# Norms of the context's keys taken during the self-attention tiles, and kept for the cross-attention tiles

## What is computed

```
q  = _ln(_fp8_linear(ln_out, wq).reshape(b, s, g, hpg, d))     # 16 heads of d=128
k  = _ln(_fp8_linear(ln_out, wk).reshape(b, s, g, d))          # 8 heads
v  = _fp8_linear(ln_out, wv)
core = _gqa(q, k, v)                                            # self attention
qx = _ln(_fp8_linear(ln_out, wqx).reshape(b, s, g, hpg, d))
kx, vx = jnp.split(einsum('bsi,oi->bso', cond, w_kv_x), 2, -1)
kx = _ln(kx.reshape(b, sc, g, d))                               # keys of the context
xout = _gqa(qx, kx, vx)                                         # cross attention
catq = _div_clamp_fp8(concat([core, xout]), proj_smooth)
x = x + tanh(g) * einsum(catq, wproj) * scale
```

## Time and profile before

| what | us |
|---|---|
| median of 3 runs | 717.38 (716.02 to 719.93) |
| the profiled execution | 718.68 |
| its span | 717.0 |
| attention part, first self score to the last cross tile's start | 204.9 to 552.6 |
| one self tile (tiles 2 to 6) | 22.7 and 23.0 in turn |
| tiles 7 and 8 | 24.9 each |
| cross tiles 9 to 14 | 22.6, 20.6, 21.2, 22.7, 21.2, 22.6 |
| busy, share of the span | PE 85%, DVE 71%, ACT 53%, POOL 51% |

### The profile page before, as it was taken

The page is one execution under the profiler, slowest core; times in us unless marked ns, Lnnn a source line. Parts: engine busy times, 40 slices in busy tenths (PEclk is TensorE's granted clock), DMA queues, the critical chain, the costliest instruction groups (busy, mean ns, idle before and its releaser), DMA issues.

```text
span 717.0 us, 10737 instructions
## 1 busy us (share of the span) xinstructions
PE 607.7 (85%) x3738; PEld 487.4 (68%) x3738; DVE 511.7 (71%) x959; ACT 380.9 (53%) x674; POOL 366.0 (51%) x306
## 2 busy tenths in 40 slices
PE   4686986589677999999997898889888989999995
PEld 2453433353455888788876787778777878888885
DVE  4679777688259689888896688998998683533333
ACT  1445767765376465655575656665665424433321
POOL 2421265000367566565667766686775643755521
PEclk9897998789699899999998969999998999999999
DMA  7950211004502010010352031220220100221001
GB/s 234 309 198 0 104 73 59 31 36 156 162 11 79 1 60 30 30 61 0 118 198 84 29 113 50 74 69 22 74 74 16 45 1 1 67 66 31 1 1 59
DMA packets 36246, 50.68 MB, mean 71 GB/s; under 512 B 8289, under 2 KB 22497, under 8 KB 36193
## 3 DMA queue, kind: packets, MB, share of 16 engines
q1 hardware_dynamic: 36192, 50.00, 21.2%
HBM read 37.41 MB, written 12.58 MB: 70 GB/s over the span
## 4 chain that ended last, share of the span: by engine, by line
PE 41%; DVE 17%; issue 10%; ACT 3%; POOL 3%; DVEq 0%; POOLq 0%; ACTq 0%
PE g_proj L2077 7%; PE g_proj L2001 6%; PE g_scores L2035 4%; DVE g_yb L1623 4%; DVE g_ve L1591 3%; PE g_turn L2024 2%; PE g_proj L457 2%; PE g_proj L458 2%; PE g_proj L459 2%; PE g_op L472 2%; PE g_op L474 2%; PE g_op L473 2%; PE g_op L2059 2%; POOL g_rs L1495 2%; DVE g_big L1641 1%
## 5 line engine op out<-in xcount | busy, mean ns | idle before, releaser
L1495 POOL TENSOR_TENSOR g_rs<-g_ve,neg_half 128x4 f32<-128x4 f32 x96 | 101.9, 1066 | 85.1 <-DVE g_ve L1591 75.4
L1591 DVE TENSOR_REDUCE g_ve<-g_sq 128x4 f32<-128x516 f32 x96 | 64.3, 680 | 41.3 <-ACT g_sq L1807 32.9
L2001 PE MATMUL g_proj<-w_hi,g_xqc 128*128 128x512 f32 x192 | 85.7, 446 | 7.9 <-POOL g_xqc L1490 6.0
L1506 POOL TENSOR_TENSOR g_cat<-g_big,g_kb 128x1024 fp32r<-128x1024 bf16 x32 | 68.3, 2134 | 39.4 <-DVE g_big L1641 39.4
L2024 PE MATMUL g_turn<-ident,g_qn 128*128 128x128 f32 x384 | 60.5, 286 | 25.0 <-DVE g_qn L1597 15.0
L2001 PE MATMUL g_proj<-w_lo,g_xqc 128*128 128x512 f32 x192 | 79.9, 416 | 0.0
L1807 ACT ACTIVATE g_sq<-g_proj 128x512 f32<-128x512 f32 x80 | 47.8, 597 | 51.6 <-PE g_proj L2001 49.3
L2035 PEld LDWEIGHTS g_scores<-g_qkT 128*128 128x128 f32 x512 | 65.1, 205 | 12.4 <-issue 11.7
L2035 PE MATMUL g_scores<-g_qkT 128*128 128x64 f32 x512 | 66.1, 286 | 7.4 <-DVE g_ex L1607 7.4
L500 POOL TENSOR_TENSOR m_h_lo<-m_h,m_h_hi 128x512 fp32r<-128x512 f32 x32 | 41.3, 1294 | 59.8 <-ACT m_h_hi L487 59.8
L2024 PEld LDWEIGHTS g_turn<-ident,g_qn 128*128 128x128 f32 x384 | 46.2, 147 | 36.9 <-DVE g_qn L1597 17.5
(11 more groups left out here) (229 smaller groups left out, 1680.4 us busy)
## 6 DMA issues: line engine op xcount, KB each, us to landing
kvx_rows<-f_kept SPq DMA_DIRECT2D x32, 256.0 KB, 2.4
g_kraw<-kvx_rows SPq DMA_DIRECT2D x16, 256.0 KB, 3.3
g_v<-kvx_rows SPq DMA_DIRECT2D x8, 512.0 KB, 4.9
m_raw<-in_L_W SPq DMA_DIRECT2D x16, 256.0 KB, 3.3
c_raw<-in_L_wqT SPq DMA_DIRECT2D x4, 512.0 KB, 9.2
f_w_ctx<-in_L_wkvxT SPq DMA_DIRECT2D x4, 512.0 KB, 7.8
x_raw<-in_L_wqxT SPq DMA_DIRECT2D x4, 512.0 KB, 3.8
c_praw<-in_L_wprojT SPq DMA_DIRECT2D x4, 512.0 KB, 6.1
```

What stands on the lines that cost most here:

```text
L1495: G.tensor_tensor(rs[:, i % 2, :], ve[:, i % 2, :], k["half"][:, 0:4], ALU.pow).then_inc(q["rs_done"], 1)
L1506: G.tensor_tensor(cat[:, h].rearrange("p h (b s) -> p b h s", b=2), big[:, h, :].rearrange("p (b h s) -> p b h s", b=2, s=SEQ), kb[:, h, : ...
L1591: V.tensor_reduce(ve[:, i % 2, :], sq[:, i % 2], AX.X, ALU.add).then_inc(q["ve_done"], 1)
L2001: last = T.matmul(bank(n, i)[:], xqc[:, n % 2, view * KT + c_, :], w[:, c_, :], start=c_ == 0 and part == 0, stop=c_ == KT - 1 and part == 1)
```

## The change

The norms of the context's keys no longer belong to the cross tiles. During self tile n = 0 to 7 the keys of context tile n are loaded once more from `kvx_rows` (512 KB in one transfer, into a new buffer `ksq`), ACT squares all eight heads in place (`key_squares`), DVE sums them (`key_sums`, into a column block of `kve`), and POOL takes the power (`key_rstd`, into `krs`), where they stay. Cross tiles norm only the four chunks of queries; their keys are still loaded and multiplied as before, by `krs`. The parity of `sq`, `ve` and `rs` now counts only chunks that are measured (`measured`), so the waits between them shift. To make room for the new buffers, `big` is gone: `lift` writes back into `yb`, and the wait on `cat_done` moves from `power` to `unload`.

```
+        ksq, kve, krs = sb("ksq", [P, KV, D + 1]), sb("kve", [P, TILES * KV]), sb("krs", [P, TILES * KV])
...
+                def norm_keys(n):
+                    if n > 0:
+                        sp.wait_ge(q["kve_done"], n)
+                    sp.dma_start(ksq[:, :, 0:D], k["kvx"][n, :, 0:2 * CH].rearrange("p (h d) -> p h d", d=D)).then_inc(q["kn_loaded"], 16)
...
                 moe.load_gates(sp, t)
+                norm_keys(0)
                 for i in range(4):
                     own_out.load(sp, t, i)
+                norm_keys(1)
...
                     ctx.load(sp, t, n)
+                    norm_keys(2 * n)
+                    norm_keys(2 * n + 1)
...
                 def rstd(n, i):
-                    after_scale(pool, n, i - 2)
+                    at = measured(n, i)
+                    measured_before(pool, n, i)
...
+                def key_rstd(n):
+                    heads = slice(n * KV, (n + 1) * KV)
+                    pool.wait_ge(q["kve_done"], n + 1)
+                    G.tensor_tensor(krs[:, heads], kve[:, heads], k["half"][:, 0:KV], ALU.pow).then_inc(q["krs_done"], 1)
...
                     m = n + 1
-                    rstd(m, 0)
+                    if not cross(m):
+                        rstd(m, 0)
...
                     fp8(n, 1)
+                    if not cross(n):
+                        key_rstd(n)
...
                 def sums(n, i):
-                    if n > 0 or i >= 2:
-                        dve.wait_ge(q["rs_done"], n * NN + i - 1)
+                    if at >= 2:
+                        dve.wait_ge(q["rs_done"], at - 1)
...
+                def key_sums(n):
+                    dve.wait_ge(q["ksq_done"], n + 1)
+                    V.tensor_reduce(kve[:, n * KV:(n + 1) * KV], ksq[:], AX.X, ALU.add).then_inc(q["kve_done"], 1)
...
+                def key_squares(n):
+                    act.wait_ge(q["kn_loaded"], 16 * (n + 1))
+                    A.activation(ksq[:, :, 0:D], ksq[:, :, 0:D], ACT.Square, scale=D ** -0.5).then_inc(q["ksq_done"], 1)
```

More of the change, by code:

```diff
@@ L1416, in after_scale, with measured, measured_before @@
                 eng.wait_ge(q["qn_done"], n * NP + (1, 2, 4, 5).index(i) + 1)
+        def measured(n, i):
+            return n * NN + i if not cross(n) else TILES * NN + (n - TILES) * NP + (1, 2, 4, 5).index(i)
+        def measured_before(eng, n, i):
+            at = measured(n, i) - 2
+            if at >= TILES * NN:
+                n, i = TILES + (at - TILES * NN) // NP, (1, 2, 4, 5)[at % NP]
+                eng.wait_ge(q["qn_done"], n * NP + (1, 2, 4, 5).index(i) + 1)
+            elif at >= 0:
+                after_scale(eng, at // NN, at % NN)
         def loads_of(n, par):
@@ L1536, in both @@
                         moe.rstd(pool, TOKENS[n])
-                    rstd(m, 3)
+                    if not cross(m):
+                        rstd(m, 3)
                     normalise(n, 1)
@@ L1680, in both_own @@
                         ctx.mean(dve, (n + 1) // 2)
+                    key_sums(n)
                     sums(m, 2)
@@ L1704, in both_cross @@
                         moe.keep_logits(dve, TOKENS[n - 1], proj[OUT_BANK])
-                    sums(m, 0)
+                    if n == TILES - 1:
+                        key_sums(n)
                     sums(m, 1)
@@ L1797, in square @@
                 def square(n, i):
-                    kind, at = CHUNKS[i]
-                    if cross(n) and kind == "k":
-                        act.wait_ge(k_loaded[at], 16 * (n - TILES + 1))
-                        source = kraw[at]
-                    else:
-                        act.wait_ge(q["qkv_done"], projected(n, i))
-                        source = bank(n, i)
-                    if n > 0 or i >= 2:
-                        act.wait_ge(q["ve_done"], n * NN + i - 1)
-                    A.activation(sq[:, i % 2, :, 0:D], source[:].rearrange("p (h d) -> p h d", d=D), ACT.Square,
-                                 scale=D ** -0.5).then_inc(q["sq_done"], 1)
@@ new lines, in scale @@
+                def scale(n, i):
+                    half = CHUNKS[i][1]
+                    if cross(n):
+                        act.wait_ge(q["krs_done"], n - TILES + 1)
+                        act.wait_ge(k_loaded[half], 16 * (n - TILES + 1))
+                        first = (n - TILES) * KV + 4 * half
+                        source, by = kraw[half], krs[:, first:first + 4]
+                    else:
+                        act.wait_ge(q["rs_done"], measured(n, i) + 1)
+                        source, by = bank(n, i), rs[:, measured(n, i) % 2, :]
@@ L1812, in scale @@
                     if n > 0 or i >= 2:
                         act.wait_ge(q["turned"], n * NN + i - 1)
-                    source = kraw[CHUNKS[i][1]] if cross(n) else bank(n, i)
                     for h in range(4):
-                        last = A.activation(qn[:, i % 2, h * D:(h + 1) * D], source[:, h * D:(h + 1) * D], ACT.Copy, scale=rs[:, i % 2, h:h + 1])
+                        last = A.activation(qn[:, i % 2, h * D:(h + 1) * D], source[:, h * D:(h + 1) * D], ACT.Copy, scale=by[:, h:h + 1])
@@ L1897, in both_cross @@
                     m = n + 1
-                    square(m, 0)
                     if cross(n):
@@ L1905, in both_cross @@
                     square(m, 2)
-                    square(m, 3)
                     scale(m, 0)
```

41 lines of the change are left out of this document (25 added, 16 removed).

## The result

| kernel | median us | runs |
|---|---|---|
| before | 717.9 | 716.0 to 719.9, 6 runs |
| after | 706.4 | 705.3 to 709.8, 6 runs |
| ratio | 0.985 | 95% interval 0.982 to 0.988 |

The forecast was 709 in a range of 702 to 716. The profiled execution of the changed kernel took 705.5, with a span of 703.4 against 717.0: 13.6 us less.

A forecast was written before the change was run, and what follows sets the result against it. No engine is full, so list order decides, with POOL late and in DVE's way: 718.68 - 2.6 - 1.1 - 4.4 + 0.7 + 1.2 + 0.2 - 2.5 = 710.2. Less 1.3 to the median: 708.9, say 709, range 702 to 716.

The forecast's parts named there:

- tiles 7 and 8: Cross tiles 7 and 8: chunk 3's power ahead of normalise goes, so PE starts turn_p earlier; 2.6 us gained.
- tiles 9 and 10: One DVE reduction leaves and the first clip is no longer hindered: 0.5 in tile 9, 0.6 in tile 10, 1.1 us gained.
- tiles 11 to 14: Reduction 0.25, clip 0.35, cat no longer late 0.69, less 0.2 for overlaps: 1.1 us a tile, 4.4 us gained.
- self tiles 2, 4, 6: Added power delays scale(m, 1) and the reduction uses up DVE's idle time: 0.26 us a tile, 0.7 us lost.
- start: One 512 KB load ahead of four others costs up to 1.5 us; with slack in the first, 0.2 us lost.
- clock: TensorE: less PE idle time removes low-clock stretches behind tiles 11, 13 and 14; up to about 5.9 us, 2.5 taken.
- rival 4: Self tiles pay: power of 2.1 and reduction of 2.2 exceed the margin in seven tiles, slower at 720; chance 0.08.
- in tile 8 PE, at a low clock, was last already: Tile 8, up to the next tile's scores: PE gains 1.0 us, without the 0.6 for DVE counted in tile 7.
- some slack: Kernel start: the first of four loads, read by ACT mid-list, had room, so 0.2 us was taken instead of 1.5.
- Rival 1: The clock stays up: all low stretches of tiles 11 to the last go, 3.4 us better, 705.5; chance 0.17.
- Rival 2: POOL's powers block DVE in tiles 11 to 14: 1.07 us a tile comes back, 713.2; chance 0.12.
- Rival 3: PE is the bound after all; DVE and POOL gains return as PE waits elsewhere, 714.2 on the median; chance 0.13.

The follow-up runs named there:

- after_awake2: Kernel after plus 24 extra PE transposes of a constant before turn_p(n, 1) of tiles 7 and 8: 704.4 us, ratio 0.981.
- before_awake2: Kernel before plus constant PE transposes: 12 before the last turn of tiles from 11 on, 24 before turn_p(n, 1) of tiles 7 and 8: 712.2 us.
- dve_sum3: Kernel after with one unused DVE reduction of 128x516 put back in each cross tile, where chunk 3's sum stood: 709.8 us, ratio 0.990.
- parity_wait: Kernel after with chunk 5's power in cross tiles again waiting until ACT has multiplied chunk 3's keys: 712.9 us, ratio 0.995.
- no_self_work: Kernel after without the added self-tile loads, squares, sums and powers; kept norms set to 1: 707.3 us, ratio 0.985.
- pool_power3: Kernel after with one unused POOL power of 128x4 put back in each cross tile, directly ahead of normalise(n, 1): 709.2 us, ratio 0.990.
- cross_back: Kernel after with unused stand-ins for the cross tiles' removed sums, powers and squares, and the wait on the key multiply: 715.1 us, ratio 0.997.
- before_awake: Kernel before plus 12 PE transposes of a constant ahead of the last turn in each tile from 11 on: 714.2 us, ratio 0.994.
- late_load: Kernel after with the first extra key load issued after the four loads of self output weights instead of ahead: 705.6 us, ratio 0.985.
- power_moved: Kernel after with each 128x8 power moved on POOL from behind cat to behind a later tile's normalise(n, 0): 708.6 us, ratio 0.985.
- all_moved: Kernel after with first load and 128x8 powers moved later, and key_sums moved ahead of each self tile's weight work on DVE: 705.6 us, ratio 0.983.
- best_awake: all_moved plus constant PE transposes before tile 1's second-half scores, a projection for tile 1, and turn_p(n, 1) of tiles 7 and 8: 698.1 us, ratio 0.973.

## Why the prediction was right, and which of its terms were not

Each term against the runs. "Clock up" is after_awake2 against before_awake2.

| step | forecast | measured | from |
|---|---|---|---|
| tiles 7 and 8 | -2.6 | -3.9 (1.89, 2.02) | clock up |
| tiles 9 and 10 | -1.1 | -0.5 (0.56, -0.03) | clock up |
| tiles 11 to 14 | -4.4 | -4.4 (1.10, 1.25, 1.07, 0.98) | clock up |
| self tiles 2, 4, 6 | +0.7 | +0.8 (0.35, 0.35, 0.07) | after_awake2, before |
| tile 0 | +1.2 | +1.1 | after, before |
| start | +0.2 | +2.1 | after, before |
| clock | -2.5 | -8.2 | the rest of 13.6, in these two executions |

Up to rounding they sum to the 13.6 us by which the profiled spans differ, with 0.5 of it ahead of the attention part. Between medians the gain was 11.5 us, where 8.4 was forecast. The path and the waits were the ones forecast, and 709 was 2.6 us off; part of that nearness is luck, since the start was 1.9 too cheap while tiles 7 and 8 (1.3) and the clock were worth more than forecast. Two sums of the forecast don't add up as written: tile 9 is entered at 0.5 although its only part, the clip, is priced 0.35, and in rival 4 a power of 2.1 and a reduction of 2.2 are 1.4 us of excess, seven times which gives about 719 and not 720.

- **Tiles 11 to 14.** All three parts were there: the reduction 0.26 (dve_sum3), the wait 0.59 against 0.69 (parity_wait), and the clip, 0.43 for 0.78. They are not three separate terms: in dve_sum3 the first clip took 0.63 in tile 13, so most of the 0.26 is the clip. The two measured parts make 0.85 of some 1.1 us a tile; no run takes the rest alone. The signs named beforehand appeared: lengths near 20.0 (20.10 to 20.21), the first clip at 0.43, `cat` waiting for `lift`, no clock under 1.00.
- **Tile 8.** I had it worth 1.0 because PE at a low clock was last there. With the clock up it is worth 2.02, nearly the same as tile 7, and in the two profiled executions, at clocks of 0.78 and 0.85, 1.90: with 24 turns in the wait on POOL the clock stayed at 1.00, so the low clock was not a property of the tile. The step "in tile 8 PE, at a low clock, was last already" failed. In the kernel after, at clocks of 0.92 and 0.85, tiles 7 and 8 took 22.37 and 23.03 where I had written 23.3 and 23.9.
- **Tile 10.** Forecast 0.6, measured none. With less in front of it, DVE's `m_xn` now starts with POOL's `normalise` beside it and takes 1.04 us for 0.38 before:

```profile
450.00 1.04 POOL L1529 TENSOR_TENSOR g_ex<-g_ex,g_rc 128x512 f32<-128x512 f32 x1 [3.31 <-DVE g_rc L1659]
```

```profile
450.15 1.04 DVE L346 TENSOR_SCALAR m_xn<-x_res,m_mv,m_rs 128x256 f32<-128x256 f32 x1 [0.23 <-issue]
```

  The new overlap took 0.66 and the 0.23 ahead of it 0.2, together what the sum and the clip gave. I had looked for new overlaps in the token split and `cat`, not in the short instruction beside `normalise`. Two runs bear the cause out. In no_self_work, with the same lists in this tile, `m_xn` starts 0.16 ahead of `normalise`, takes 0.38, and tile 10 takes 20.01 us for 20.61: the forecast 0.6. In dve_sum3 a sum more stands in the list, `m_xn` takes 0.38, and the tile is shorter than in the kernel after (20.34).

```profile
451.00 0.38 DVE L346 TENSOR_SCALAR m_xn<-x_res,m_mv,m_rs 128x256 f32<-128x256 f32 x1
```

- **Start.** Forecast 0.2 with a bound of 1.5. Starts with the load where the change puts it took 24.1 to 25.6 us from POOL's first instruction of the attention part to the first self maximum (after, pool_power3, dve_sum3, cross_back, after_awake2), those without it or with it later 23.2 to 23.4 (no_self_work, before_awake, late_load). In runs with one long low stretch instead the two groups are 22.7 and 22.2 (parity_wait and power_moved; before, all_moved and best_awake); before_awake2, with the shortest low stretch, took 21.2. So the load costs 0.5 to about 1, beside the wait of 1.01 on ACT, and the rest of the 2.1 is where the low stretches fell in the two executions. My "some slack" was the mis-sized word: the row of four transfers gave a median of 6.1, and the first one is not the median. With the load ahead of them the same median is 8.4 (kernel after), with it behind them 6.3 (late_load): about 2.2 more, not the 1.5 of the forecast's bound.
- **The clock.** The mechanism was the one named; its size is less sure than the row of the table. Rival 1 came true in tiles 11 to 14 of the profiled execution: it has no low stretch from 419 to 571 us, worth 1.4 in tile 12 and 1.4 in tile 14. But only tiles 7 to 14 have runs that hold the change to account. They took 180.64 us before and 174.38 with the clock up, 167.17 after and 165.54 with the clock up: 6.3 us of low clock became 1.6, so 4.6 less. The low stretch that the kernel before has at 551 us, behind the 1.50 us at the end of tile 14, is gone too; before_awake, without it, took 163.1 for 164.4 in the last part, so 1.3 of the 2.8 there goes with it. The rest of the 8.2 is mostly the other 1.5 of the last part and tile 1 (1.7), less tiles 2 and 6 (1.1), and these vary as much between runs with the same lists there: 25.55 to 27.02 us in tile 1 of the six other kernels that keep the changed lists in it, 159.95 to 163.10 in the last part of the ten others with it as in the kernel after. The medians give less again: the change gains 11.5 us, and 7.9 with the turns in both kernels, so about 3.6 for the clock, an estimate with an error of some us. That the forecast of 2.5 was too low is likely; that it was off by 5.7 is not shown.
- **Rival 2.** POOL's power ran from 473.87 to 474.94 beside the clip at 474.01, and the clip took its 0.43. It did not block. By the rule of the Trainium skill ("SBUF — State Buffer", "SBUF: two separate sides"), an exclusive lock for the whole instruction, the clip would have waited until 474.94; the rule is for some kinds of DVE instruction only, and no run here shows whether the clip is one. The token split at 474.84 did hold back the instruction at 474.93 (0.65 for 0.43), and `normalise` held `m_xn`; there the trace agrees with the rule.
- **Rival 3.** PE's idle time at the last turn fell from 1.51 to 0.56, not to nothing; it did not become the bound in these tiles. **Rival 4.** The power and the reduction came out at 1.64 and 1.22; its point of 1.3 us excess a tile was never near. The cost of tiles 2, 4 and 6 came as worked out, by POOL's power ahead of two others, as power_moved shows.

**Open.** Why single executions of one kernel differ in which tiles run at the low clock, and why the same idle time of PE is followed by a low stretch in one tile and not in the next; so also why late_load and power_moved, which mend what they are made for, show nothing in the median. Nor are the 3 us fully settled by which the median of pool_power3 stands above the kernel after; a power that waits for a real sum, which would have cost in tiles 11 to 14 too, was not tried.

## What to carry to other kernels

Price a removed wait twice: once as the wait, once as the low TensorE clock that can follow the same idle time; in tiles 7 to 14 the lists were worth 8.8 us here and the clock 4.6 more in the profiled executions. When one unit of work is dropped, redo the lists' overlaps around it: what moves earlier can meet another neighbour and give the gain back, as `m_xn` did. And compare two versions with the clock held up in both, by harmless turns in PE's waits: that tells the terms apart, and is itself worth keeping.

## What was not expected of the hardware

- Work that computes nothing pays: 96 extra turns of a constant took all_moved from 705.6 to 698.1 us (medians of two sets, whose kernel before stood at 718.1 and 717.2).
- The clock did not follow the busy share of a tile. Tile 11 of before, at 1.00, ended with 1.51 us of idle PE and tile 12 had the low stretch; tile 10 had ended with 0.90 us and no low stretch followed, nor did one follow 1.56 us at the end of tile 12. cross_back had one behind 1.29 but none behind 1.30 two tiles later, parity_wait none behind 1.16 in four tiles, and the kernel after none behind 0.56.
- POOL's power grows with the numbers in a partition: 0.55 us for 1, 1.07 for 4, 1.64 for 8. And in tile 11 after it ran beside a DVE clip that took its usual 0.43, while the same kind of clip took 1.31 to 2.15 beside `cat`, a POOL instruction of 2.12 us with two full inputs.
- The eight loads of 512 KB, one transfer each, had a median of 4.4 us to landing. The first of them, ahead of the four loads of output weights, made ACT wait 1.01 us.
